# Attention by two key tiles: scores in runs of three, two and three, and a third place for the probabilities

## The chip, the cores and the metric

The kernel runs on one core of one Trainium2 chip. The metric is the device time of one execution in microseconds, the median of several; lower is better. A separately profiled execution gives the trace that the rows below are read from.

## The reference, cut to what matters

One transformer layer on x of 2 x 1024 x 256, float32: half a feed-forward block (with a product-key expert part), then attention with 16 heads of width 16, then half a feed-forward block again. The change is in the attention:

```python
q, k, v = (_split(lora_linear(layernorm(x), W, b, Bm, Am)) for each of q, k, v)   # 2 x 16 x 1024 x 16
scores = jnp.einsum('bhqd,bhkd->bhqk', q, k) * 16 ** -0.5
attn = jax.nn.softmax(scores, axis=-1)
out = jnp.einsum('bhqk,bhkd->bhqd', attn, v)
x = x + lora_linear(out, Wo, bo, Bo, Ao)
```

## The kernel before

The heads are taken two at a time: 16 groups (g) of two heads (j = 0, 1), eight groups for each of the two batches. A group has 1024 queries and 8 key tiles (kt) of 128 keys.

**Stacks.** For every head, q and k are split into a high and a low float32r part and stacked into 48 rows, so that one matmul over 48 rows gives an exact enough score. Head 0's rows stand in partitions 0 to 48, head 1's in partitions 64 to 112, so that matmuls of the two heads use different halves of TensorE's rows. Row 49 of each (index 48) is one row more: minus the maximum of the query on q's side, ones on k's side. So the maximum of each query must be known before the scores proper of its group can be computed.

**Max pairs.** The maxima of group g + 1 are prepared during group g. `max_scores(g, m)` computes one of 16 pairs: two matmuls (`max_pair`, L1595), head 1 and then head 0, each 128 queries by 512 keys, into two banks of `max_ps`. VectorE then takes the maximum over both banks in one instruction (`take_maxima`, L1865). `max_ps` holds two pairs, so pair m may start when the reduce of pair m - 2 has ended (the wait on `pair_max`, L1602). `ahead(g, step)` issues pair step + EARLY of the coming group; EARLY is 6.

**Scores.** `score(g, i)` (L1635) is one of 32 matmuls of a group: 128 keys by 512 queries, i // 4 the key tile, i % 2 the head. It writes one of three banks, the ring (`score_ps`, RING = 3): element n waits for ScalarE to have emptied element n - 3 (`ring_slot`). ScalarE's `exponential` (L1785) turns a bank into probabilities in `probs`, which has two places, one for each key tile.

**Value products.** `mix(g, kt, part)` (L1654) multiplies values and probabilities of a key tile for half of the queries. It is four float32 matmuls with 32 columns of weights and 256 moving columns each, which take one quarter of TensorE's columns each; the trace shows eight, since each float32 matmul is issued as two. `mixed_ps` sums them over the eight key tiles. After the last key tile ScalarE copies it out (`copy_mixed`, L1790), and the first value product of the next group waits for that copy.

**The order on TensorE** is written out by hand. A key tile kt of group g is

```python
score(g, 4 * kt)
ahead(g, 2 * kt)
score(g, 4 * kt + 1)
mix(*divmod(g * KEY_TILES + kt - 1, KEY_TILES), 0)
score(g, 4 * kt + 2)
ahead(g, 2 * kt + 1)
score(g, 4 * kt + 3)
mix(*divmod(g * KEY_TILES + kt - 1, KEY_TILES), 1)
```

so half a key tile is a run of four wide matmuls (score of head 0, max pair head 1, max pair head 0, score of head 1) and then four value products. In front of some key tiles stand other ring elements: the transposes of the group before (`turn_out`, L1623, at kt 2), the turn of the maxima (`turn_group_max`, L1616, at kt 6), and from group 9 on the output projection of the first batch (`attention_rows` at kt 3, `output_product`, L356, at kt 5). In the last group the turns and routing rows of the second feed-forward stand there too. The other engines follow the same order, the ring's by `PLACE`, a table made from `ring_order`.

**Weights.** The weights of the second feed-forward are fetched again during the attention into `weights_again` (L208, on the SP queue) and split by GpSimd (L233, L235); that tensor has two places of 1024 columns.

Of the kernel before, what the change touches and what calls it, by code (L numbers as in the profile page):

```python
# [152 lines left out]
class FfnWeights:  # L153
# [61 lines left out]
    def raw_again(self, i, places):  # L215
        place = places[:, i % 2, :]
        if self.AGAIN[i].startswith("late"):
            return place[:, 0:CHUNK]
        return place.rearrange("p (k f) -> p k f", k=KT)
# [194 lines left out]

class LastMix:
# [13 lines left out]
    def copy_on_scalar(self, act, bank):  # L429
        act.wait_ge(self.turned, 1)  # L430
        act.wait_ge(self.group_out, 2 * (GROUPS - 2))
        act.activation(self.rows.rearrange("p t a b -> p (t a b)"), bank, ACT.Copy).then_inc(self.copied, 1)
# [906 lines left out]
def attention_block(nc, block, sem, dram, keep, attn, proj, norm, halves, weights, project, later, later_space):  # L1339
# [4 lines left out]

    KEY_TILES = SEQ // P
    STRIP = 32
    PAIRS = 2 * KEY_TILES
    SCORES = KEY_TILES * 2 * 2
    EARLY, EARLY_IN_FRONT = 6, 4
    RING, PROBS = 3, 2  # L1350
    OUT_TURN_AT, MAX_TURN_AT = 2, 6
    COPY_AFTER = 3
    UPDATE_AT, TURN_ROWS_AT, PRODUCT_AT = 5, 3, 5
    FIRST_PAIR_AT = 9
    NORM_PAIRS = JT // 2
    LATER_TURNS, LATER_ROWS = (1, 2, 3, 4), (3, 4, 5, 6)

    def ring_order():
# [3 lines left out]
        for g in range(GROUPS):  # L1362
            for kt in range(KEY_TILES):
                if kt == OUT_TURN_AT and g:
                    yield "out", g - 1
                if kt == MAX_TURN_AT and g < GROUPS - 1:
                    yield "max", g + 1
                if (g, kt) == (FIRST_PAIR_AT - 1, UPDATE_AT):
                    yield "update", 0
                if kt == TURN_ROWS_AT and 0 <= g - FIRST_PAIR_AT < NORM_PAIRS:  # L1370
                    yield "rows", g - FIRST_PAIR_AT
                if kt == PRODUCT_AT and 0 <= g - FIRST_PAIR_AT < NORM_PAIRS:
                    yield "product", g - FIRST_PAIR_AT
                for i in range(4 * kt, 4 * kt + 4):
# [18 lines left out]
    with ExitStack() as scope:  # L1393
# [13 lines left out]
        again = sb("weights_again", [P, 2, KT * HALF_INTER], F32)  # L1407
# [6 lines left out]
        turned = sb("turned", [P, 2, KEY_TILES // 2, 4, STRIP], F32)  # L1414
# [173 lines left out]
        def _(pe):  # L1588
# [97 lines left out]
            def ahead(g, step):  # L1686

                later, m = divmod(step + EARLY, PAIRS)
                if g + 1 + later < GROUPS:
                    max_scores(g + 1 + later, m)  # L1690
# [16 lines left out]
            def first_key_tile():  # L1707
                for half in range(2):
                    score(0, 2 * half)
                    max_scores(1, EARLY_IN_FRONT + 2 * half)  # L1710
                    score(0, 2 * half + 1)
                    value_rows(TILES - 2 + half)
                    max_scores(1, EARLY_IN_FRONT + 2 * half + 1)
# [18 lines left out]
            for m in range(EARLY_IN_FRONT):  # L1732
# [3 lines left out]
                value_rows(10 + m)  # L1736
            for g in range(GROUPS):
                for kt in range(KEY_TILES):
                    if kt == OUT_TURN_AT and g:
                        turn_out(g - 1)  # L1740
                    if kt == MAX_TURN_AT and g < GROUPS - 1:
                        turn_group_max(g + 1)
                    if (g, kt) == (FIRST_PAIR_AT - 1, UPDATE_AT):
                        out = ring_slot(PLACE["update", 0])
                        pe.wait_ge(project.raw_in, 48)
                        project.update_on_tensor(pe, out).then_inc(ring_in, 1)
                    if kt == TURN_ROWS_AT and 0 <= g - FIRST_PAIR_AT < NORM_PAIRS:
                        attention_rows(g - FIRST_PAIR_AT)
# [253 lines left out]
```

## Time and profile before

| | |
|---|---|
| Median of 3 runs | 835.8 us (833.98 to 836.37) |
| Profiled execution, its own time | 834.09 us |
| Its span in the trace | 832.3 us |
| TensorE matmul busy | 807.2 us, 97% of the span |
| VectorE busy | 684.2 us, 82% |
| ScalarE busy | 472.6 us, 57% |
| Reduces of max pairs (L1865) | 256, 311.1 us busy, 29.7 us idle before them |
| Exponentials (L1785) | 512, 277.2 us busy, 39.3 us idle before them |

Busy time is a sum over the span. The first feed-forward and the projections fill about the first 270 us, the attention the next 355, the second feed-forward the rest. A matmul's bar in the trace has a modelled end, so what counts on TensorE are the distances from start to start.

### The profile page before, as it was taken

The page shows a single profiled execution, that of the slowest core. Times are in us where ns is not written, and L with a number is a line of the kernel's source. Part 1 is how long each engine was busy: PE and PEld are TensorE (multiplying, and loading weights), DVE is VectorE, ACT ScalarE, POOL GpSimd, SP SyncE. Part 2 cuts the span into 40 slices and gives each one's busy share as a digit, 9 for nine tenths or more (in the row PEclk, how much of TensorE's full clock was granted, in tenths as well). Part 3 has the DMA queues.
Part 4 walks back from the last instruction along what each step waited for, and adds up shares of the span by engine and source line. Part 5 has one row for each costly group of instructions (what it writes and reads, how often), then busy time and mean ns, then how long its engine had stood idle before and what let it go on. Part 6 is the DMA issues. An engine that isn't in the chain of part 4 may idle for free.

```text
span 832.3 us, 14311 instructions
## 1 busy us (share of the span) xinstructions
PE 807.2 (97%) x5424; PEld 516.6 (62%) x5424; DVE 684.2 (82%) x1130; ACT 472.6 (57%) x897; POOL 189.5 (23%) x203
## 2 busy tenths in 40 slices
PE   5989999999999999999999999999999999999997
PEld 4868788887876433333333444443358888888886
DVE  5998798787699999999999988889846977876865
ACT  4444333342442788888888888888863333333322
POOL 2450212021011033333332421143430201120100
PEclk9999999999999999999999999999999999999999
DMA  8110000000050242223333222210000000000000
GB/s 288 41 27 1 0 1 1 1 2 0 1 90 1 40 78 54 40 39 65 65 65 64 41 39 40 57 35 26 15 14 1 1 2 26 0 26 1 1 25 26
DMA packets 19333, 27.87 MB, mean 33 GB/s; under 512 B 4608, under 2 KB 13632, under 8 KB 19264
## 3 DMA queue, kind: packets, MB, share of 16 engines
q1 hardware_dynamic: 18784, 26.40, 14.4%
q8 instruction: 43, 0.70, 0.4%
q10 hardware_dynamic: 480, 0.56, 0.3%
q14 instruction: 26, 0.21, 0.1%
HBM read 12.09 MB, written 2.10 MB: 17 GB/s over the span
## 4 chain that ended last, share of the span: by engine, by line
PE 85%; DVE 8%; ACT 4%; issue 2%; DMA 1%; DVEq 0%; ACTq 0%; POOL 0%
PE front_ps L1654 16%; PE front_ps L1635 13%; PE max_ps L1595 6%; PE ffn_gate_ps L48 5%; PE ffn_gate_ps L50 5%; PE ffn_gate_ps L49 5%; PE ffn_out_ps L741 5%; PE ffn_out_ps L742 5%; PE ffn_out_ps L745 5%; PE ffn_up_ps L48 3%; PE ffn_up_ps L49 3%; PE ffn_up_ps L50 3%; ACT probs L1785 2%; PE ffn_mix_ps L720 2%; DVE ffn_hidden_lo L1103 1%
## 5 line engine op out<-in xcount | busy, mean ns | idle before, releaser
L1865 DVE TENSOR_REDUCE maxima<-max_ps 128x2 f32<-128x1024 f32 x256 | 311.1, 1223 | 29.7 <-PE max_ps L1595 26.9
L1785 ACT ACTIVATE probs<-front_ps 128x512 f32<-128x512 f32 x512 | 277.2, 597 | 39.3 <-PE front_ps L1635 29.5
L873 ACT ACTIVATE ffn_tanh<-ffn_gate_ps 128x512 f32<-128x512 f32 x96 | 57.4, 598 | 227.5 <-PE ffn_gate_ps L50 227.5
L1654 PE MATMUL front_ps<-probs,values 128*32 128x256 f32 x2048 | 163.4, 391 | 4.5 <-ACT mixed_t L1790 4.0
L1112 DVE SCALAR_TENSOR_TENSOR ffn_gated<-ffn_tanh,ffn_gate_ps 128x512 f32<-128x512 f32 x96 | 65.7, 685 | 61.6 <-ACT ffn_tanh L873 61.2
L1654 PEld LDWEIGHTS front_ps<-probs,values 128*32 128x32 f32 x2048 | 40.8, 107 | 95.3 <-issue 55.7
L1635 PE MATMUL front_ps<-q_stack,k_stack 49*128 49x512 f32 x256 | 94.7, 446 | 0.0
L1595 PE MATMUL max_ps<-ffn_xlo,ffn_xhi 48*128 48x512 f32 x256 | 93.8, 447 | 0.0
L1635 PE MATMUL front_ps<-ffn_xhi,ffn_xlo 49*128 49x512 f32 x256 | 91.6, 456 | 0.0
L1535 POOL TENSOR_TENSOR inverse_sum<-turned,minus_one 128x16 f32<-128x16 f32 x15 | 43.7, 2912 | 207.6 <-ACT turned L1797 207.6
L1595 PE MATMUL max_ps<-k_stack,q_stack 48*128 48x512 f32 x256 | 88.2, 455 | 0.6 <-DVE maxima L1865 0.4
L48 PE MATMUL ffn_gate_ps<-ffn_xhi,block 128*128 128x512 f32 x192 | 78.1, 407 | 1.4 <-DVE ffn_xlo L1014 1.4
L741 PE MATMUL ffn_out_ps<-ffn_hidden_hi,block 128*128 128x512 f32 x192 | 78.9, 411 | 0.0
L50 PE MATMUL ffn_gate_ps<-ffn_xlo,block 128*128 128x512 f32 x192 | 76.0, 396 | 0.0
L49 PE MATMUL ffn_gate_ps<-ffn_xhi,block 128*128 128x512 f32 x192 | 75.7, 394 | 0.0
L742 PE MATMUL ffn_out_ps<-ffn_hidden_hi,block 128*128 128x512 f32 x192 | 75.1, 391 | 0.0
L1103 DVE TENSOR_TENSOR ffn_hidden_lo<-ffn_hidden,ffn_hidden_hi 128x512 fp32r<-128x512 f32 x96 | 72.6, 757 | 0.2
L1635 PEld LDWEIGHTS front_ps<-q_stack,k_stack 49*128 49x128 f32 x256 | 39.0, 185 | 47.3 <-ACT probs L1785 43.9
L1635 PEld LDWEIGHTS front_ps<-ffn_xhi,ffn_xlo 49*128 49x128 f32 x256 | 38.1, 184 | 47.1 <-ACT probs L1785 39.0
L956 POOL TENSOR_TENSOR ffn_mix<-ffn_row_exp,ffn_expo 128x512 f32<-128x512 f32 x32 | 34.5, 1099 | 139.7 <-DVE ffn_row_exp L1080 139.7
L879 ACT ACTIVATE ffn_hidden_hi<-ffn_hidden 128x512 fp32r<-128x512 f32 x96 | 59.8, 623 | 3.4 <-DVE ffn_hidden L1124 1.9
L745 PE MATMUL ffn_out_ps<-ffn_hidden_lo,block 128*128 128x512 f32 x192 | 59.6, 391 | 1.4 <-DVE ffn_hidden_lo L1103 1.4
(205 smaller groups left out, 1287.0 us busy)
## 6 DMA issues: line engine op xcount, KB each, us to landing
q_stack<-block SPq DMA_DIRECT2D x48, 64.0 KB, 2.3
ffn_xhi<-block SPq DMA_DIRECT2D x48, 64.0 KB, 2.3
ffn_xlo<-block SPq DMA_DIRECT2D x48, 64.0 KB, 2.3
k_stack<-block SPq DMA_DIRECT2D x42, 64.0 KB, 2.3
x_sb<-in_x SPq DMA_DIRECT2D x3, 512.0 KB, 9.0
out<-x_sb SPq DMA_DIRECT2D x3, 512.0 KB, 2.9
ffn_out_rows<-in_down SPq DMA_DIRECT2D x4, 256.0 KB, 6.2
weights_again<-in_gate SPq DMA_DIRECT2D x2, 512.0 KB, 3.6
```

Of the source, the lines that this page charges most:

```text
L48: pe.matmul(out, w_hi, x_hi, start=(k == 0), stop=False)
L49: pe.matmul(out, w_lo, x_hi, start=False, stop=False)
L50: done = pe.matmul(out, w_hi, x_lo, start=False, stop=(k == last))
L741: pe.matmul(out_ps[:, k, :], weights.late_hi(piece)[:, at], x_hi, start=(m == 0), stop=False)
L742: pe.matmul(out_ps[:, k, :], weights.late_lo(piece)[:, at], x_hi, start=False, stop=False)
L745: out = pe.matmul(out_ps[:, k, :], weights.late_hi(piece)[:, at], x_lo, start=False, stop=(m == UNITS - 1))
L1103: v.tensor_tensor(hidden_lo[:, u % SPLIT_RING, :], hidden[:, u % HIDDEN_RING, :], hidden_hi[:, u % SPLIT_RING, :].bitcast(F32), ALU.subtra ...
L1595: return pe.matmul(max_ps[:, m % 2, j, :], q_stack[s][rows, qt * P:(qt + 1) * P], k_stack[s][rows, half * HALF:(half + 1) * HALF], start=T ...
L1635: pe.matmul(out, k_stack[s][rows, kt * P:(kt + 1) * P], q_stack[s][rows, half * HALF:(half + 1) * HALF], start=True, stop=True).then_inc(r ...
L1654: mm = pe.matmul(mixed_ps[strip:strip + STRIP, at:at + HALF // 2], values[g % SLOTS][:, kt, j, :], probs[:, (g * KEY_TILES + kt) % PROBS, ...
L1785: act.activation(probs[:, tile % PROBS, j, half * HALF:(half + 1) * HALF], score_ps[:, n % RING, :], ACT.Exp, scale=SCORE_SCALE).then_inc( ...
L1865: v.reduce_max(maxima[:, g % 2, m // 2, m % 2, :], max_ps[:, m % 2, :, :], axis=AXIS_X).then_inc(pair_max, 1)
```

## The change

The attention is now issued by two key tiles at a time (`two`, four of them in a group). The eight scores of two key tiles stand in runs of three, two and three. One max pair is split at each of the two inner borders: its head 1 matmul ends a run and its head 0 matmul begins the next, so that the runs have six, four and six wide matmuls. A value product of four stands behind the first and the second run, and two of them (of the first of the two key tiles) behind the third. `probs` has three places. The other ring elements stand in front of the run of two. EARLY is 8 instead of 6. To make room, `turned` is stored with 17 columns of each strip of 32 (ScalarE's copies read only those), and `weights_again` has one place for the four wide pieces and two for the narrow ones, so a wide piece is fetched when the one before it is split.

```diff
@@ load_again, sp
-        if i >= 2:
-            sp.wait_ge(self.again_lo, i - 1)
+        if i:
+            sp.wait_ge(self.again_lo, i if i <= 4 else max(i - 1, 4))
@@ used_columns (new), and its use
+def used_columns(bank):
+    return bank.rearrange("p (s x) -> p s x", x=STRIP)[:, :, 0:HD + 1]
...
-                act.activation(turned[:, g % 2, :, :, :].rearrange("p t a b -> p (t a b)"), score_ps[:, n % RING, :],
-                               ACT.Copy).then_inc(ring_out, 1)
+                act.activation(turned[:, g % 2, :, :, :].rearrange("p t a b -> p (t a) b"),
+                               used_columns(score_ps[:, n % RING, :]), ACT.Copy).then_inc(ring_out, 1)
@@ constants and storage
-    EARLY, EARLY_IN_FRONT = 6, 4
-    RING, PROBS = 3, 2
-    OUT_TURN_AT, MAX_TURN_AT = 2, 6
-    COPY_AFTER = 3
-    UPDATE_AT, TURN_ROWS_AT, PRODUCT_AT = 5, 3, 5
+    EARLY, EARLY_IN_FRONT = 8, 5
+    RING, PROBS = 3, 3
+    TWOS = KEY_TILES // 2
+    TURN_ROWS_AT, OUT_TURN_AT, MAX_TURN_AT, PRODUCT_AT = range(TWOS)
+    UPDATE_AT = PRODUCT_AT
...
-    LATER_TURNS, LATER_ROWS = (1, 2, 3, 4), (3, 4, 5, 6)
+    LATER_TURNS, LATER_ROWS = (2, 4, 6, 8), (5, 7, 9, 10)
...
-        again = sb("weights_again", [P, 2, KT * HALF_INTER], F32)
+        again = sb("weights_again", [P, KT, HALF_INTER], F32)
...
-        turned = sb("turned", [P, 2, KEY_TILES // 2, 4, STRIP], F32)
+        turned = sb("turned", [P, 2, KEY_TILES // 2, 4, HD + 1], F32)
@@ the order of the ring
+            for two in range(TWOS):
+                for i in range(8 * two, 8 * two + 3):
+                    yield "score", (g, i)
...
-                for i in range(4 * kt, 4 * kt + 4):
+                for i in range(8 * two + 3, 8 * two + 8):
                     yield "score", (g, i)
@@ TensorE
-            def max_scores(g, m):
-                if m == 0:
+            def max_scores(g, m, heads=(1, 0)):
+                if g >= GROUPS:
+                    return
+                if m == 0 and 1 in heads:
                     pe.wait_ge(stacks_in[g % SLOTS], (g // SLOTS + 1) * STACK_DMAS * 16)
-                if g * PAIRS + m >= 2:
+                if g * PAIRS + m >= 2 and 1 in heads:
                     pe.wait_ge(pair_max, g * PAIRS + m - 1)
-                max_pair(g, m, 1)
-                max_pair(g, m, 0).then_inc(pair_scored, 1)
+                for j in heads:
+                    scored = max_pair(g, m, j)
+                    if j == 0:
+                        scored.then_inc(pair_scored, 1)
...
+            def two_key_tiles(g, two):
+                i, step, last_group = 8 * two, 4 * two, g == GROUPS - 1
+                tile = g * KEY_TILES + 2 * two
+                score(g, i)
+                ahead(g, step)
+                score(g, i + 1)
+                score(g, i + 2)
+                ahead(g, step + 1, (1,))
+                if last_group:
+                    run_later(3 * two)
+                mix(*divmod(tile - 1, KEY_TILES), 0)
+                between(g, two)
+                ahead(g, step + 1, (0,))
+                score(g, i + 3)
+                score(g, i + 4)
+                ahead(g, step + 2, (1,))
+                if last_group:
+                    run_later(3 * two + 1)
+                mix(*divmod(tile - 1, KEY_TILES), 1)
+                ahead(g, step + 2, (0,))
+                score(g, i + 5)
+                score(g, i + 6)
+                ahead(g, step + 3)
+                score(g, i + 7)
+                if last_group:
+                    run_later(3 * two + 2)
+                mix(g, 2 * two, 0)
+                mix(g, 2 * two, 1)
```

`between` holds the calls of `turn_out`, `turn_group_max`, `attention_rows` and `output_product` that stood in the loop, each now with its own `two`: the rows of the output projection at 0, the turn of the group before at 1, the turn of the maxima at 2, the product and the update of its weights at 3. `run_later` holds those of the second feed-forward. The first two key tiles of group 0 are written out in a new function `first_two`, which mixes their eight scores with seven max pairs and the last two value-row products; five max pairs of group 1 now stand in front of it where four stood before. ScalarE takes its work in the new ring order, with `copy_mixed` behind the exponential of score 4 of a group.

## Rows read from the trace of the kernel before

**Rows 1.** Busy time in one group; columns: window, its length, busy us (instructions) by engine

```profile
338.85:359.86 21.01, 20.73 (x199) 8.11 (x197) 19.59 (x18) 18.44 (x35) 6.73 (x5) 1.00 0.24 40
```

**Rows 2.** Chain that ended last, 317 to 341 us; start, length, what

```profile
317.88 1.09 ACT probs L1785 x2
...
338.85 1.08 ACT probs L1785 x2
```

**Rows 3.** Timeline of TensorE's matmuls, 355.55 to 358.10 us; start, length, what

```profile
355.61 0.50 PE L1635 MATMUL front_ps<-ffn_xhi,ffn_xlo 49*128 49x512 f32 x1
355.61 0.73 PE L1595 MATMUL max_ps<-k_stack,q_stack 48*128 48x512 f32 x2
355.95 0.40 PE L1635 MATMUL front_ps<-ffn_xhi,ffn_xlo 49*128 49x512 f32 x1
356.28 0.64 PE L1654 MATMUL front_ps<-probs,values 128*32 128x256 f32 x8
356.85 0.50 PE L1635 MATMUL front_ps<-ffn_xhi,ffn_xlo 49*128 49x512 f32 x1
```

**Rows 4.** Timeline of TensorE's weight loads, the same stretch

```profile
355.72 0.19 PEld L1635 LDWEIGHTS front_ps<-ffn_xhi,ffn_xlo 49*128 49x128 f32 x1
```

**Rows 5.** Groups of instructions by shape, 300 to 440 us; busy, mean ns, idle before

```profile
L1865 DVE TENSOR_REDUCE maxima<-max_ps 128x2 f32<-128x1024 f32 x107 | 130.1, 1223 | 8.7 <-PE max_ps L1595 7.6
L1785 ACT ACTIVATE probs<-front_ps 128x512 f32<-128x512 f32 x214 | 116.1, 596 | 14.9 <-PE front_ps L1635 10.5
```

**Rows 6.** Timeline of TensorE's matmuls, 274.6 to 275.6 us, group 0's first key tile

```profile
274.97 0.62 PE L1635 MATMUL front_ps<-q_stack,k_stack 49*128 49x512 f32 x2
...
275.52 0.39 PE L1302 MATMUL front_ps<-wv_hi,ffn_xhi 128*128 128x256 f32 x1
```

**Rows 7.** Timeline of TensorE's matmuls, 623.9 to 625.7 us, end of the attention

```profile
624.24 1.07 PE L1654 MATMUL front_ps<-probs,values 128*32 128x256 f32 x16 [0.42 <-ACT probs L1785]
625.24 0.50 PE L48 MATMUL ffn_gate_ps<-ffn_xhi,block 128*128 128x512 f32 x1
```

**Rows 8.** Timeline of VectorE in two windows, around 277 us and 288 us

```profile
276.31 1.22 DVE L1865 TENSOR_REDUCE maxima<-max_ps 128x2 f32<-128x1024 f32 x1
...
288.38 2.35 DVE L1865 TENSOR_REDUCE maxima<-max_ps 128x2 f32<-128x1024 f32 x2
```

**Rows 9.** Timeline of TensorE (272.5 us on) and of VectorE (270.4 us on)

```profile
272.54 0.73 PE L1595 MATMUL max_ps<-k_stack,q_stack 48*128 48x512 f32 x2
...
273.31 1.22 DVE L1865 TENSOR_REDUCE maxima<-max_ps 128x2 f32<-128x1024 f32 x1 [0.33 <-PE max_ps L1595]
```

**Rows 10.** Timeline of TensorE's weight loads, 276.2 to 278.3 us

```profile
276.44 0.19 PEld L1595 LDWEIGHTS max_ps<-k_stack,q_stack 48*128 48x128 f32 x2 [0.15 <-DVE maxima L1865]
...
277.58 0.18 PEld L1595 LDWEIGHTS max_ps<-k_stack,q_stack 48*128 48x128 f32 x2 [0.83 <-DVE maxima L1865]
```

**Rows 11.** Timeline of weight loads and of matmuls, 588.3 to 589.8 us

```profile
588.70 0.18 PEld L1635 LDWEIGHTS front_ps<-ffn_xhi,ffn_xlo 49*128 49x128 f32 x1
...
589.12 0.64 PE L1654 MATMUL front_ps<-probs,values 128*32 128x256 f32 x8
```

**Rows 12.** Timeline of TensorE's matmuls at the border of two groups, 339.8 us on

```profile
339.90 0.40 PE L1635 MATMUL front_ps<-ffn_xhi,ffn_xlo 49*128 49x512 f32 x1
340.57 0.64 PE L1654 MATMUL front_ps<-probs,values 128*32 128x256 f32 x8 [0.28 <-ACT mixed_t L1790]
```

**Rows 13.** Timeline of TensorE's matmuls, 592.1 us on, key tile 5 of group 14

```profile
592.17 0.50 PE L1635 MATMUL front_ps<-ffn_xhi,ffn_xlo 49*128 49x512 f32 x2
...
594.41 0.28 PE L1616 MATMUL front_ps<-ident,maximum 128*16 128x128 f32 x1
```

**Rows 14.** Instructions on `weights_again`; duration ns min/median/max, first and last start

```profile
L235 POOL TENSOR_TENSOR block<-weights_again,block x12: 1278/1282/2378, 391.2 to 611.9; 128x512 fp32r<-128x512 f32 x8, 128x1024 fp32r<-128x1024 f32 x4
L208 SPq DMA_DIRECT2D weights_again<-in_gate x2: 437/437/437, 375.9 to 396.9; - x2
```

More of the change, by code:

```diff
@@ L215, in raw_again @@
     def raw_again(self, i, places):
[L216 to L219, printed above, removed]
+        return places[:, i % 2, :] if self.AGAIN[i].startswith("late") else places[:, :, :]
     def wait_again(self, pe, piece):
@@ L431, in copy_on_scalar @@
         act.wait_ge(self.group_out, 2 * (GROUPS - 2))
-        act.activation(self.rows.rearrange("p t a b -> p (t a b)"), bank, ACT.Copy).then_inc(self.copied, 1)
+        act.activation(self.rows.rearrange("p t a b -> p (t a) b"), used_columns(bank), ACT.Copy
+                       ).then_inc(self.copied, 1)
     def write_on_vector(self, v):
@@ L1684, in rows_later, with ahead @@
                              .rearrange("p h k -> p (h k)"))
-            def ahead(g, step):
+            def ahead(g, step, heads=(1, 0)):
                 later, m = divmod(step + EARLY, PAIRS)
-                if g + 1 + later < GROUPS:
-                    max_scores(g + 1 + later, m)
+                max_scores(g + 1 + later, m, heads)
             def product(m):
@@ L1705, in value_rows, with first_two @@
                 proj.value_rows_on_tensor(pe, t, front_bank("rows", t // 2))
[L1707 to L1713, printed above, removed]
+            def first_two():
+                early = iter(range(EARLY_IN_FRONT, EARLY + 4))
+                score(0, 0)
+                max_scores(1, next(early))
+                score(0, 1)
+                score(0, 2)
+                max_scores(1, next(early))
+                value_rows(TILES - 2)
+                max_scores(1, next(early))
+                score(0, 3)
+                score(0, 4)
+                max_scores(1, next(early))
+                value_rows(TILES - 1)
+                max_scores(1, next(early))
+                score(0, 5)
+                max_scores(1, next(early))
+                score(0, 6)
+                max_scores(1, next(early))
+                score(0, 7)
+                mix(0, 0, 0)
+                mix(0, 0, 1)
@@ new lines, in run_later, with between @@
+            def run_later(run):
+                if run in LATER_TURNS:
+                    turn_later(LATER_TURNS.index(run))
+                if run in LATER_ROWS:
+                    rows_later(LATER_ROWS.index(run))
+            def between(g, two):
+                if two == OUT_TURN_AT and g:
+                    turn_out(g - 1)
+                if two == MAX_TURN_AT and g < GROUPS - 1:
+                    turn_group_max(g + 1)
+                if (g, two) == (FIRST_PAIR_AT - 1, UPDATE_AT):
+                    out = ring_slot(PLACE["update", 0])
+                    pe.wait_ge(project.raw_in, 48)
+                    project.update_on_tensor(pe, out).then_inc(ring_in, 1)
+                if two == TURN_ROWS_AT and 0 <= g - FIRST_PAIR_AT < NORM_PAIRS:
+                    attention_rows(g - FIRST_PAIR_AT)
+                if two == PRODUCT_AT and 0 <= g - FIRST_PAIR_AT < NORM_PAIRS:
+                    output_product(g - FIRST_PAIR_AT)
@@ L1850, in _ @@
                         ring_copy(("product", r), project.rows[:, (r + 1) % 2, :])
-                    for i in range(4 * kt, 4 * kt + 4):
+                    exponential(g, 8 * two + 3)
+                    exponential(g, 8 * two + 4)
+                    if two == 0 and g:
+                        copy_mixed(g - 1)
+                    elif two == 0:
+                        value_rows(7)
+                    for i in range(8 * two + 5, 8 * two + 8):
                         exponential(g, i)
-                        if i == COPY_AFTER and g:
-                            copy_mixed(g - 1)
-                        elif i == COPY_AFTER:
-                            value_rows(7)
             copy_mixed(GROUPS - 1)
```

61 lines of the change are left out of this document (19 added, 42 removed).

## The prediction

> **What bounds the kernel now.** I read the busy time by stage first, then the chain that ended last, then the timeline of one steady stretch. Within a group of the attention TensorE is busy 20.73 of 21.01 us, VectorE 19.59, ScalarE 18.44 [rows 1]: three engines near full, so a gain on one is small unless the others follow. The chain runs from group to group in 20.97 us (317.88 to 338.85) [rows 2] and passes through TensorE, save once a group through two exponentials and the copy. VectorE waits for TensorE 7.6 us in 140 [rows 5]. So TensorE sets the pace.
>
> Half a key tile takes 1.24 us, 355.61 to 356.85 [rows 3]. The matmuls of the two heads stream together; I call two such a slot. The first slot starts at 355.61, the second 0.34 later at 355.95, because its weights are only loaded from 355.72 on [rows 4]; the value products start 0.33 after that and the next run 0.57 after them. Two key tiles are four such halves, 4.96 us; 16 halves are 19.84 of the group's 20.97. The rest, 1.13, is the wait of the first value product for `copy_mixed`, which starts 0.67 after the slot in front of it instead of 0.33 [rows 12], so 0.34, and 0.79 for the turns.
>
> **TensorE's side of the change.** A third slot in a run starts 0.23 after the second (the second of two scores starts at 0.62 - 0.39), while another shape starts 0.32 after the last slot [rows 6]. A run of six is thus 0.34 + 0.23 + 0.33 = 0.90, the run of four 0.67. One value product stays 0.57; two in a row are 1.00 (624.24 to 625.24) instead of 1.14 [rows 7]. Two key tiles: 0.90 + 0.57 + 0.67 + 0.57 + 0.90 + 1.00 = 4.61 us, 0.35 less than 4.96.
>
> A rule that agrees: by the Trainium skill, TensorEngine Tiling (Array Packing), Key Properties, going from one tiling mode to another drains the engine, and the change has three such exchanges where there were four. By that rule alone the change is worth what TensorE saves.
>
> **VectorE's side.** The reduces need 1.13 us from start to start when nothing is late (2.35 - 1.22) [rows 8], 4.52 for the four of two key tiles. That is under 4.61, but with 2% to spare and only two places, and now the pairs no longer come evenly. Let c be the start of the third run. It begins with head 0 of the third pair, the fourth pair stands at its end, so both are scored within 0.5 us; then comes none until the next run's second slot. The second pair is opened at the end of the first run and closed only behind the value products, and holds a place for that time.
>
> The hand-overs: a reduce starts 0.04 after the matmul's bar ends (272.54 + 0.73 = 273.27, reduce at 273.31) [rows 9], so 0.54 after the start of a first slot (bar 0.50). A freed place is used 0.05 after the reduce's end (276.31 + 1.22 = 277.53, load at 277.58) [rows 8, 10]. A matmul whose weight load comes late, in the middle of a run, holds the next shape back until 0.42 after that load (588.70 to 589.12) [rows 11].
>
> The chain of waits then closes on itself. From c: 0.54 to the third pair's reduce, 1.13 to the fourth's, 1.22 to its end, 0.05 to the load of head 1 of the next second pair (which needs the fourth's place), 0.42 to the value products, 0.57 to the run of two, and 0.67 + 0.57 = 1.24 to the next c. The sum is 5.17 us, against 4.61 without it. TensorE would want that load 2.36 after c (0.34 + 0.23 + 0.33 + 1.00 for the third run and its products, 0.46 into the next) and gets it at 2.94.
>
> A second loop goes through the other waits. From the run of two, b: 0.54 + 1.22 + 0.05 until head 1 of the fourth pair may load, 0.11 for that load (355.61 to 355.72) [rows 3, 4], 0.23 + 0.33 + 1.00 to the next period, 0.34 + 0.43 to its first pair's reduce, 1.22 + 0.05 until the next third pair may load, 0.42 + 0.57 to c: 6.51. With c to b by the first loop (3.93) that is 10.44 for two periods, 5.22. I take T = 5.20 for two key tiles; the bounds are 5.12 (the hand-overs at their shortest) and 5.30.
>
> A rule that bears on it: by the Trainium skill, TensorEngine Tiling (Array Packing), PSUM Bottleneck, packing speeds up TensorE and not the emptying of PSUM, which can become the bottleneck. It speaks against the change in the same sense as the loops.
>
> **The other edits.** `copy_mixed` now has the third run to hide behind: its copy (0.60, like an exponential [rows 5]) ends before the two value products at c + 0.90, so the 0.34 goes; uncovered it costs 0.34 again. The turns and the output projection keep their matmuls and still follow a value product: 0.79 a group and unchanged elsewhere. The third place of `probs` takes a wait from ScalarE, which is not late: 8 exponentials at 0.49 (1.09 - 0.60) [rows 2, 5] are 3.92 of 5.2. The narrower copy of the turns shortens work off the path; nothing to 0.2 us a group, taken as nothing. The single wide place of `weights_again`: a split that starts at 391.2 ends at 393.6, and the next load is issued at 396.9 [rows 14], so SP waits for nothing; if it did, the stacks of a group three ahead stand behind it. Front: seven pairs in `first_two` at 1.13 are 7.9 us for VectorE, but VectorE is idle before them now (0.33 and more [rows 9]) and a pair is moved ahead; between -0.6 and +2.3 (two pairs more), taken as 0.
>
> **Sum.** A new group is 4 x 5.20 + 0.79 = 21.59 against 20.97: +0.62, times 13 groups, +8.1. Group 0 has three such periods instead of six key tiles at 2.48: +0.7. At the end, pairs are needed until key tile 4 of group 14 now and until 3 with EARLY 8; after that a key tile without pairs takes 2.24 (592.17 to 594.41) [rows 13]. New, a period without pairs is bound by the ring: from c, 0.54 + 2 x 0.49 + 0.60 + 0.05 until score 2 of the next may load, 0.42 + 0.57 + 0.42 + 0.57, is 4.15, and about 0.2 for score 4, which waits for the exponential of score 1: 4.35. Now: 5 x 2.48 + 11 x 2.24 + 2 x 0.34 = 37.7; new: 2 x 5.20 + 6 x 4.35 = 36.5; -1.2. In all +7.6, or 57 T - 288.8 in general. The profiled execution took 834.1, so 842; it is 1.7 below the median 835.8, which goes to 843.5. I forecast 844.
>
> **Rivals.**
> Faster: TensorE's saving arrives, because VectorE's waits overlap and only its sum counts. T = 4.61, 57 T - 288.8 = -26, 810 us. For it: 4.52 is under 4.61, and TensorE is the bound. Against it: program order. It decides if the first loop is under 5.02; it is 5.17 by eight rows, and no single one is off by 0.15 likely. 15%. The rule on the drain is on this side.
> No change: the late load costs only its lateness, since the slot's weights would be exposed in part anyway; 0.33 instead of 0.42 in each loop gives about 5.08, +0.8, 837 us. 11%.
> Slower still: the ring's waits add to those of the pairs, as in the stretch without pairs (0.2 a period): T = 5.40, +19, 855 us. For it: three scores in a row want all three banks. Against it: ScalarE has 1.3 us to spare in each period. 12%.
> The forecast itself: 62%, its own range 840 to 849.
>
> **Numbers.** A measurement here tells about 0.3%, 2.5 us, from no change. Faster 15%, same 11%, slower 62 + 12 = 74%. The range goes from 831 (some way into the first two rivals) to 853.
>
> **What the profile would show.** Between groups 21.6 us on the chain instead of 20.97, with VectorE's reduces on it, which are not on it now. TensorE idle, or its weight loads waiting for the reduces, at two places of a period: in front of the value products of the first run and in the third run, about 0.5 us and 0.3 us. A third slot 0.23 behind the second. No wait for `copy_mixed`. The reduces in twos: third and fourth back to back at 1.13, the second alone. Periods of 4.6 us would prove me wrong; so would a weight load of a pair that starts before the reduce that frees its place, or a stretch without pairs that is not faster.

## The result and the profile after

The changed kernel takes 845.8 us (median of 4, 843.84 to 847.09), the kernel before, on the same chip, 834.9: a ratio of 1.0132, with a 95% interval of 1.0115 to 1.0150, so 11 us slower. Its profiled execution took 846.68 us, its span is 844.9.

The page of the changed kernel first: the span, the busy time by engine, the chain by engine, and the groups of the reduces and of the exponentials.

```profile
span 844.9 us, 14310 instructions
PE 822.4 (97%) x5424; PEld 546.9 (65%) x5424; DVE 678.6 (80%) x1130; ACT 463.7 (55%) x897; POOL 189.7 (22%) x203
...
PE 87%; DVE 8%; issue 2%; ACT 1%; DMA 1%; DVEq 0%; ACTq 0%; POOL 0%
...
L1923 DVE TENSOR_REDUCE maxima<-max_ps 128x2 f32<-128x1024 f32 x256 | 306.6, 1221 | 43.7 <-PE max_ps L1604 37.5
L1839 ACT ACTIVATE probs<-front_ps 128x512 f32<-128x512 f32 x512 | 271.8, 601 | 59.3 <-PE front_ps L1648 56.0
```

The work is the same (256 reduces of 1.22 us), but VectorE now sits idle 37.5 us for the max matmuls, where it was 26.9 us in the kernel before:

```profile
L1865 DVE TENSOR_REDUCE maxima<-max_ps 128x2 f32<-128x1024 f32 x256 | 311.1, 1223 | 29.7 <-PE max_ps L1595 26.9
```

Where TensorE's time went shows in the chain of the stretch of 315 to 345 us. Its columns are start, length and what; shown are the pair of value products that ends a period of two key tiles, and, one group on, every piece of the period up to the next such pair.

```profile
320.12 1.00 PE front_ps L1667 x16
...
336.57 1.00 PE front_ps L1667 x16
337.57 0.43 PE front_ps L1648
338.00 0.24 PE max_ps L1604 x2
338.24 0.24 PE front_ps L1648 x2
338.48 0.29 PE max_ps L1604
338.77 0.57 PE front_ps L1667 x8
339.34 0.43 PE max_ps L1604
339.76 0.23 PE front_ps L1648 x2
339.99 0.05 PE max_ps L1604
340.04 0.57 PE front_ps L1667 x8
340.61 0.42 PE max_ps L1604
341.04 0.24 PE front_ps L1648 x2
341.27 0.31 PE max_ps L1604 x2
341.58 0.23 PE front_ps L1648
341.81 1.00 PE front_ps L1667 x16
```

A group is 341.81 - 320.12 = 21.69 us, against 20.97 [rows 2]; a period without turns is 341.81 - 336.57 = 5.24. No reduce stands on this chain: it puts the lost time down to `max_ps` on TensorE. The busy time of one group, in the window view, hides it too:

```profile
318.10:339.80 21.70, 21.70 (x199) 10.09 (x197) 19.35 (x17) 17.85 (x35) 6.73 (x5) 1.00 0.22 38
```

TensorE is busy 21.70 of 21.70, where it was 20.73 of 21.01 [rows 1]: the modelled bars of its matmuls cover the gaps. The gaps show in the distances from start to start, and their cause in the weight loads and in VectorE's lane. This is the timeline of the next period, TensorE's matmuls, then its loads, then VectorE:

```profile
342.74 0.50 PE L1648 MATMUL front_ps<-ffn_xhi,ffn_xlo 49*128 49x512 f32 x1
343.09 0.61 PE L1648 MATMUL front_ps<-ffn_xhi,ffn_xlo 49*128 49x512 f32 x2
343.91 0.64 PE L1667 MATMUL front_ps<-probs,values 128*32 128x256 f32 x8
344.48 0.50 PE L1604 MATMUL max_ps<-k_stack,q_stack 48*128 48x512 f32 x1
345.22 0.64 PE L1667 MATMUL front_ps<-probs,values 128*32 128x256 f32 x8
345.79 0.50 PE L1604 MATMUL max_ps<-k_stack,q_stack 48*128 48x512 f32 x1
346.96 0.64 PE L1667 MATMUL front_ps<-probs,values 128*32 128x256 f32 x8
...
343.48 0.18 PEld L1604 LDWEIGHTS max_ps<-k_stack,q_stack 48*128 48x128 f32 x1 [0.21 <-DVE maxima L1923]
344.79 0.18 PEld L1604 LDWEIGHTS max_ps<-k_stack,q_stack 48*128 48x128 f32 x1
346.29 0.19 PEld L1604 LDWEIGHTS max_ps<-k_stack,q_stack 48*128 48x128 f32 x2 [0.21 <-DVE maxima L1923]
...
341.07 3.66 DVE L1923 TENSOR_REDUCE maxima<-max_ps 128x2 f32<-128x1024 f32 x3
345.01 2.54 DVE L1923 TENSOR_REDUCE maxima<-max_ps 128x2 f32<-128x1024 f32 x2 [0.28 <-PE max_ps L1604]
```

The run of three and a head, 342.74 to its value products at 343.91, takes 1.17 us instead of the 0.90 of the sum; the run of two, 344.48 to 345.22, 0.74 instead of 0.67; the third run, 345.79 to 346.96, 1.17 instead of 0.90. These 0.61 us are the difference between the 4.61 of TensorE alone and the 5.22 that a period takes. Each of the three late loads begins 0.05 to 0.06 behind the end of a reduce: 341.07 + 1.14 + 1.22 = 343.43 and 343.48 (the second of three in a row, which started 1.14 behind the first), 341.07 + 3.66 = 344.73 and 344.79, 345.01 + 1.22 = 346.23 and 346.29. The value products stand 0.43 behind two of these loads (343.48 to 343.91, 344.79 to 345.22), and 0.67 behind the one that has a slot of scores behind it (346.29). The waits of 290 to 620 us, with columns of total, times and longest, say the same in two directions, and none is for `mixed_t`:

```profile
DVE maxima L1923 <- PE max_ps L1604: 37.0, 56, 2.2
...
PEld max_ps L1604 <- DVE maxima L1923: 25.4, 111, 0.3
```

**Where the 12.6 us lie** (spans 844.9 and 832.3; by the starts of the first score of each group in the two traces). 1.85 lie ahead of the first max pair, in instructions that both kernels share; that point falls between 240.1 and 243.5 us over the kernels below, so it is scatter of one execution. From the first pair of group 1, which is scored in front of group 0, to the second period of group 0 (the front): +1.6, 14.48 for 12.86. Rest of group 0: +0.8. Groups 1 to 13: +8.9, 0.685 each. Group 14 +0.3, group 15 -0.6, after the attention -0.2.

### The profile page after: what moved, and what is told of

It reads as the page before. It is cut to its first block, busy times and chain, and to the rows that moved or that the text cites. A ratio compares the mean times of both kernels' runs of the same rounds, so it can differ in the third digit from the quotient of the medians.

```text
span 844.9 us, 14310 instructions
## 1 busy us (share of the span) xinstructions
PE 822.4 (97%) x5424; PEld 546.9 (65%) x5424; DVE 678.6 (80%) x1130; ACT 463.7 (55%) x897; POOL 189.7 (22%) x203
## 4 chain that ended last, share of the span: by engine, by line
PE 87%; DVE 8%; issue 2%; ACT 1%; DMA 1%; DVEq 0%; ACTq 0%; POOL 0%
PE front_ps L1667 16%; PE max_ps L1604 12%; PE front_ps L1648 11%; PE ffn_gate_ps L48 5%; PE ffn_gate_ps L50 5%; PE ffn_gate_ps L49 5%; PE ffn_out_ps L747 5%; PE ffn_out_ps L748 4%; PE ffn_out_ps L751 4%; PE ffn_up_ps L50 3%; PE ffn_up_ps L48 3%; PE ffn_up_ps L49 3%; PE ffn_mix_ps L726 2%; DVE ffn_hidden_lo L1109 1%; DVE maxima L1923 1%
## 5 line engine op out<-in xcount | busy, mean ns | idle before, releaser
L1923 DVE TENSOR_REDUCE maxima<-max_ps 128x2 f32<-128x1024 f32 x256 | 306.6, 1221 | 43.7 <-PE max_ps L1604 37.5
L1839 ACT ACTIVATE probs<-front_ps 128x512 f32<-128x512 f32 x512 | 271.8, 601 | 59.3 <-PE front_ps L1648 56.0
L1667 PE MATMUL front_ps<-probs,values 128*32 128x256 f32 x2048 | 150.1, 388 | 0.4 <-ACT probs L1839 0.4
L1667 PEld LDWEIGHTS front_ps<-probs,values 128*32 128x32 f32 x2048 | 47.0, 108 | 67.9 <-issue 33.9
L1648 PE MATMUL front_ps<-q_stack,k_stack 49*128 49x512 f32 x256 | 90.2, 434 | 0.0
L1648 PE MATMUL front_ps<-ffn_xhi,ffn_xlo 49*128 49x512 f32 x256 | 87.9, 443 | 0.2 <-ACT probs L1839 0.2
L1604 PEld LDWEIGHTS max_ps<-ffn_xlo,ffn_xhi 48*128 48x128 f32 x256 | 37.7, 184 | 36.5 <-issue 20.4
L1604 PEld LDWEIGHTS max_ps<-k_stack,q_stack 48*128 48x128 f32 x256 | 34.8, 183 | 36.0 <-issue 18.3
```

The costliest lines, as they stand in the source:

```text
L1604: return pe.matmul(max_ps[:, m % 2, j, :], q_stack[s][rows, qt * P:(qt + 1) * P], k_stack[s][rows, half * HALF:(half + 1) * HALF], start=T ...
L1648: pe.matmul(out, k_stack[s][rows, kt * P:(kt + 1) * P], q_stack[s][rows, half * HALF:(half + 1) * HALF], start=True, stop=True).then_inc(r ...
L1667: mm = pe.matmul(mixed_ps[strip:strip + STRIP, at:at + HALF // 2], values[g % SLOTS][:, kt, j, :], probs[:, (g * KEY_TILES + kt) % PROBS, ...
L1839: act.activation(probs[:, tile % PROBS, j, half * HALF:(half + 1) * HALF], score_ps[:, n % RING, :], ACT.Exp, scale=SCORE_SCALE).then_inc( ...
L1923: v.reduce_max(maxima[:, g % 2, m // 2, m % 2, :], max_ps[:, m % 2, :, :], axis=AXIS_X).then_inc(pair_max, 1)
```

## The experiments

Ratios are to the kernel before, timed on the same chip in turn. Group times are from the first score of a group to that of the next, groups 1 to 7.

### 1. Half of each reduce, with the new order and with the old

The maxima are taken over half of the columns, so the output is not the reference's; everything else is issued as it was. One edit, made in the changed kernel (`after_half_reduce`) and in the kernel before (`before_half_reduce`):

```diff
-                v.reduce_max(maxima[...], max_ps[:, m % 2, :, :], axis=AXIS_X
+                v.reduce_max(maxima[...], max_ps[:, m % 2, :, 0:HALF // 2], axis=AXIS_X
```

> The changed kernel with each reduce of a max pair over half of the columns (256 of 512 in each bank); the maxima leave out half of the keys. A reduce then takes about 0.69 us instead of 1.22. If the reduces' two loops set the period of two key tiles (5.2 us), both fall below TensorE's own sum and the period becomes 4.61: 26 us under the kernel before by the formula of the prediction, about 809 us, a group near 19.2 us, and no weight load of a max pair waits for VectorE. If the ring of three score banks or TensorE's own split runs set it, the period stays above 5 us and the time above 832 us.

> The kernel before with the same halved reduces (the maxima leave out half of the keys), as a control. VectorE does not set its period, so the reduces' theory says no change: 835 us within 2 us, half a key tile at 1.24 us as before. If the reduces cost time there too, it falls by several us.

Measured: changed kernel 822.7 us, ratio 0.9859 (0.9846 to 0.9873); kernel before 833.3, ratio 0.9993 (0.9979 to 1.0006). A group of the changed kernel fell from 21.69 to 19.75, the group of the kernel before did not move (20.97 and 20.96). No weight load of a pair waits for VectorE any more in the changed kernel between 300 and 440 us, as expected. The chain of the changed kernel with short reduces, 290 to 400 us:

```profile
314.87 1.00 PE front_ps L1667 x16
319.51 1.00 PE front_ps L1667 x16
...
329.50 1.00 PE front_ps L1667 x16
334.62 1.00 PE front_ps L1667 x16
```

A period without turns is 319.51 - 314.87 = 4.64, close to the 4.61 summed for TensorE; 329.50 to 334.62, with 0.21 of a turn in it, is 4.91 without that turn, and the one at the group's border 4.76. Those two wait for the ring (for the turn of the maxima, and for ScalarE, which copies `mixed`); that in the changed kernel the waits for the reduces cover this is an inference, and experiment 6 fits it. So the reduces carry the loss within the groups: the old order does not wait for them there, the new one does. In front of them both orders wait: with short reduces the front of the kernel before falls from 12.86 to 11.91 us, about the 1 us by which its total fell, and that of the changed kernel from 14.48 to 12.66. The total missed the expected 809 by 14 us, for the ring, and for one more thing, told under what was unexpected.

### 2. Whole pairs, and one whole pair

`whole_pairs` keeps the new runs but scores both heads of every pair together, behind the value product; `second_pair_whole` does that for the second pair of a period alone (the first two lines of the edit).

```diff
-                ahead(g, step + 1, (1,))
...
-                ahead(g, step + 1, (0,))
+                ahead(g, step + 1)
...
-                ahead(g, step + 2, (1,))
...
-                ahead(g, step + 2, (0,))
+                ahead(g, step + 2)
```

> The changed kernel with both split pairs whole at the start of the next run: runs of five, four and seven wide matmuls. The second pair no longer asks for its place before the fourth's reduce has ended, the third none before the first's. TensorE needs nine slots instead of eight, 4.61 + 0.23 = 4.84 us; the head 1 matmul of the fourth pair may still come 0.1 late. Reduce theory: period 4.84 to 4.95, a group about 20.4 us, 826 to 831 us, faster than both kernels. If split pairs do not matter and the extra slot only adds, the period is 5.2 + 0.23 and the time about 858 us. If the ring sets the period, no change from 846 us.

> The changed kernel with only one of its two split pairs whole again: both matmuls of the second pair of maxima of a period stand behind the first run's value products, those of the third pair stay on either side of the second run's. My theory, two loops of waits of about equal length (5.17 and 5.22 us a period), of which this edit opens the one that runs through the second pair and loosens the other: a period of about 5.1, a group of 21.2, and 838 to 840 us in all. Rival A (only the second loop, through the third pair, binds): groups stay at 21.6 and the time at 845. Rival B (only the first binds): groups as with both whole, 20.8, and 835 us.

Measured: `whole_pairs` 834.5 us, ratio 0.9999 (0.9989 to 1.0009), a group of 20.77; `second_pair_whole` 841.0 us, 1.0075 (1.0061 to 1.0088), a group of 21.36. Whole pairs take the loss away, but the 826 to 831 us and the gain over the kernel before that were expected did not come: the group is 0.4 above the expected 20.4, and the front stays as long as in the changed kernel (14.45). With whole pairs the loads' waits for the reduces fall to 5.6 us in the stretch of 300 to 440 us, from 12.0. Undoing both splits gives 0.92 a group back, undoing one 0.33: neither rival with one loop alone holds (21.6 or 20.8), and the total of the second is 1 us above the range that was given.

### 3. Whole pairs with half of each reduce

The edits of 1 and 2 together. The first set:

> whole_pairs with each reduce over half of the columns (the maxima leave out half of the keys). Theory: in whole_pairs nine slots of TensorE (4.84 us) set the period, with about 0.1 of lateness of the fourth pair. So the group falls from 20.77 only to about 20.4 us and the time by some 3 to 5 us to 830, where the same halving took 23 us off the changed kernel. If the reduces still set the period of whole_pairs, it falls by 10 us or more.

It gave 839.5 to 859.9 us and once 2597. The second set, of the same kernel:

> The changed kernel with whole pairs and with half of each reduce left out (the maxima are taken over half of the keys' scores), once more, unchanged: its first set lay between 839 and 2597 us and gives no verdict. With the reduces out of the way only TensorE's own order and the ring's waits are left. My theory: 4.62 + 0.11 for the slot more, and the same ring waits as in after_half_reduce, a group of about 20.1 and 829 us. Rival (whole pairs cost more than a slot by themselves): over 833. Rival (order does not matter without reduces): 823.

Measured: 858.6 us, ratio 1.0292. The total was missed by 30 us, 28 of them in groups 0 to 2 (93.6 us in place of some 65.7), at a lower clock (below). From group 3 on the group is 20.60, against the 20.1 expected, which had put the slot more at 0.11 a period; it takes 0.21 (a period without turns and without the group's border is 4.85, 422.80 to 427.65 on its chain, against 4.64). That completes a table of group times:

| us a group | pairs split | pairs whole |
|---|---|---|
| reduces of 1.22 us | 21.69 | 20.77 |
| reduces of 0.69 us | 19.75 | 20.60 |

The split is worth 0.85 a group to TensorE (0.21 a period: whole pairs make runs with an odd number of wide matmuls, and the one left over takes a slot of its own) and costs 0.92 where a pair is opened in one run and closed in the next while VectorE needs 1.22 us for each. The same edit is a gain or a loss by the length of the reduce.

### 4. The storage alone

The kernel before with three places of `probs`, the narrow `turned` and the single wide place of `weights_again`.

```diff
-    RING, PROBS = 3, 2
+    RING, PROBS = 3, 3
...
-        again = sb("weights_again", [P, 2, KT * HALF_INTER], F32)
+        again = sb("weights_again", [P, KT, HALF_INTER], F32)
...
-        turned = sb("turned", [P, 2, KEY_TILES // 2, 4, STRIP], F32)
+        turned = sb("turned", [P, 2, KEY_TILES // 2, 4, HD + 1], F32)
```

> The kernel before with the storage edits alone: three places of probabilities, the turned rows at 17 columns a strip, one wide place for the weights fetched again; the order is that of before. Theory: none of them is on the path, 835 us within 2 us. Rival: the narrower copies of the turns or the third place are worth something by themselves (up to 0.2 us a group, 3 us in all), or the single place makes SP late and costs time.

Measured: 834.5 us, ratio 1.0001 (0.9990 to 1.0012), a group of 20.96. Nothing, as forecast.

### 5. The old order, with one new period a group

The storage of experiment 4, the front and EARLY of the kernel before, and only the first two key tiles of a group in runs of three, two and three; `copy_mixed` one score later. In `hybrid_whole` the pairs there are whole, in `hybrid_split` split.

```diff
+            def first_key_tiles(g):
+                score(g, 0)
+                ahead(g, 0)
+                score(g, 1)
+                score(g, 2)
+                mix(g - 1, KEY_TILES - 1, 0)
...
+                ahead(g, 1)
+                score(g, 3)
+                score(g, 4)
+                mix(g - 1, KEY_TILES - 1, 1)
+                ahead(g, 2)
+                score(g, 5)
+                score(g, 6)
+                ahead(g, 3)
+                score(g, 7)
+                mix(g, 0, 0)
+                mix(g, 0, 1)
...
-                        if i == COPY_AFTER and g:
+                        if i == COPY_AFTER + 1 and g:
```

> The order of the kernel before with its storage edits (three places of probabilities), except that the first two key tiles of groups 1 to 15 are issued in the layout of whole_pairs (runs of five, four and seven wide matmuls, value products behind the first two and two behind the third, copy_mixed behind the exponential of score 4). Theory: the only lasting gain in the change is that copy_mixed has a run to hide behind. There the two key tiles take 4.95 us as measured in whole_pairs instead of 4.96 + 0.34, so a group 20.6 us instead of 20.97, 15 times 0.35 is 5 us: 829 to 830 us where before takes 834.5. Rival: the change of layout within a group costs the reduces as much at the border, and nothing changes (834 us).

> As hybrid_whole, but with the two pairs split at the inner borders as in the change (runs of six, four and six). Reduce theory: head 1 of the second pair comes 0.35 us late and head 1 of the fourth 0.34 (each counted from the reduce that frees its place, as in the prediction), so these two key tiles take about 5.27 us, hardly less than the 5.30 of before: 833 to 835 us, and 4 to 5 us more than hybrid_whole in spite of a slot less. If splitting is harmless and only TensorE's slots count, it is the faster of the two by 15 times 0.23, 3.5 us.

> The kernel hybrid_whole once more, unchanged, for a profile of it and a second set of times (its first set gave 829.1 to 832.0 us, with a first execution of 4212 us in which every matmul took some 1.75 us where it takes 0.4 elsewhere). My theory: the groups from 1 on run as in whole_pairs, 20.77 us (no wait of TensorE for the copy of mixed, a wait of some 0.2 a period for the reduces), and the front runs as in before, so the time is 830 to 832 us, 0.4 to 0.6% under before. Rival (the first set was chance): 834 to 835.

Measured: `hybrid_whole` 830.9 us over five executions (a sixth took 4212 us), ratio 0.9950 (0.9936 to 0.9964), and in the second set 830.0, ratio 0.9944 (0.9929 to 0.9958); `hybrid_split` 833.7, ratio 1.0000 (0.9988 to 1.0012). `hybrid_whole` is the only version here that computes what the reference does and beats both kernels. The second set's chain of `hybrid_whole`, 290 to 400 us, at the borders of groups:

```profile
297.87 1.01 PE front_ps L1659 x16
...
318.49 1.01 PE front_ps L1659 x16
```

A group is 20.62 (20.63 by most of the first scores), 0.34 less than 20.97: just the wait for `mixed_t` [rows 12], which the new runs hide. The new period itself takes 4.96 without the turn in it, what two old key tiles take. With the pairs split the group is 20.95: the loads' waits for the reduces, 2.8 us in the stretch of 300 to 440 us against 1.3 with whole pairs and none in the kernel before, take the same 0.3 back, in one period of four.

### 6. More work for ScalarE

The changed kernel with a copy of 128x48 behind every second exponential, to find out whether the ring's waits bound it.

```diff
+                if i % 2:
+                    if g or i > 1:
+                        act.wait_ge(scratch_set, g * SCORES // 2 + i // 2)
+                    act.activation(scratch[:, :], attn["ident"][:, 0:48], ACT.Copy).then_inc(scratch_set, 1)
```

> The changed kernel with a small copy of 48 columns more on ScalarE behind every second exponential (four in two key tiles, some 0.2 us each), which nothing reads. Reduce theory: ScalarE has 1.3 us to spare in a period of 5.2, so 846 us within 2 us. Ring theory (the waits for ScalarE's banks add to those for the reduces): each of them comes straight behind an exponential and holds the next back, 0.2 us a period or more, 11 us: 857 us.

Measured: 847.4 us, ratio 1.0152 (1.0139 to 1.0165), a group of 21.81: 0.12 more than the changed kernel, for 16 copies a group of some 0.24 us each. ScalarE has room, and the rival in which the ring adds to the pairs' waits falls.

### 7. Two pairs less ahead

EARLY is 6 again, and the turn of the maxima and the output product change places.

```diff
-    EARLY, EARLY_IN_FRONT = 8, 5
+    EARLY, EARLY_IN_FRONT = 6, 3
...
-    TURN_ROWS_AT, OUT_TURN_AT, MAX_TURN_AT, PRODUCT_AT = range(TWOS)
+    TURN_ROWS_AT, OUT_TURN_AT, PRODUCT_AT, MAX_TURN_AT = range(TWOS)
...
                if m < 4:
                    value_rows(10 + m)
+            value_rows(13)
```

> The changed kernel with the maxima two pairs less ahead: EARLY 6 instead of 8, three pairs of group 1 in front of the first scores instead of five, and the turn of the maxima moved to the last two key tiles of a group (the product of the output projection takes its place in the third). My theory: of the 12.5 us by which the changed kernel's span is longer, some 2.4 lie between the first pair of group 1 and the end of group 0, because VectorE's reduces are back to back there; two pairs less in front take 2 x 1.13 = 2.3 off, one half period at the end goes back to the pace with pairs (+0.4): 844 us, between 843 and 845, the groups at 21.7 as in the changed kernel. Rival A (the front is bound by TensorE's order in the first two key tiles, not by the reduces): 846 to 847. Rival B (the place of the turn of the maxima matters for the pace, since the two ring elements now stand otherwise): groups off 21.7 by more than 0.2 and a total off by 3 us or more.

Measured: 853.9 us, ratio 1.0214 (1.0194 to 1.0233). The expectation failed: 8 us more than the changed kernel, not less. The groups 1 to 4 are 22.0, groups 5 to 7 are 23.3 to 25.6, and group 13 is 24.7 (21.67 in the changed kernel). By these numbers rival B is nearest, but what the traces show is another cause than the place of the turn. The stretch ahead of group 1 did what was expected of it by half: from the first pair of group 1 to the start of group 1 it takes 29.19 us, the changed kernel 30.36 and the kernel before 27.94, so two pairs give back 1.2 of the 2.4. The chain of this kernel, 310 to 345 us:

```profile
330.21 1.24 DVE maxima L1924
...
331.47 0.03 DVE maximum L1931
...
331.85 2.35 DVE maxima L1924 x2
...
334.25 0.49 PE max_ps L1604
```

After the 16 reduces of a group VectorE takes the larger of each two maxima in one small instruction (`maximum`, L1931 here). With the pairs two less ahead it stands between the second and the third pair of a period. The reduce behind it starts 0.38 later (331.47 to 331.85), another follows without a gap, and the load of the next second pair, at 334.25, stands 0.05 behind their end (331.85 + 2.35 = 334.20). The turn comes 1 us behind that late load. The last period of a group takes 0.3 more than in the changed kernel, where the same instruction costs 0.14 (332.80 to 332.94) behind the fourth pair. And the instruction is not always short. In group 5, on VectorE and then on GpSimd, which splits weights of the second feed-forward:

```profile
397.49 1.56 DVE L1931 TENSOR_TENSOR maximum<-maxima 128x16 f32<-128x16 f32 x1
...
396.62 2.38 POOL L232 TENSOR_TENSOR block<-weights_again,block 128x1024 fp32r<-128x1024 f32 x1
```

It takes 0.19 us with nothing on GpSimd beside it, 0.45 to 0.47 beside another instruction of GpSimd in groups 1 to 4, and 1.56 to 1.58 in groups 5 to 7 and 1.27 in group 13, each time begun inside a split of weights. These are the four stretched groups. In group 5 the granted clock is 1.00 up to 400 us, and 0.80 and then 0.73 only behind it, from 400 to 407 us, so the lower clock follows this wait and does not lead to it. That GpSimd's work makes the instruction long is read from the overlap alone; no run took it away. The place of the turn and the lead of the pairs were moved together, so this run does not price either alone, and nothing in it shows a cost of the turn's place.

## Why the prediction came out right

Forecast 844 us, 840 to 849 by its own range; measured 845.8. The change itself was forecast at 8.2 us (844 less 835.8) and measured at 10.9 (845.8 less 834.9); that the totals lie only 1.8 apart is in part luck, since the kernel before came out 0.9 lower in this comparison.

**TensorE's side** holds. The third slot stands 0.23 behind the second (of the two scores at 343.09 the second starts 0.61 less one bar of 0.39 later, 0.22), two value products take 1.00 (336.57 to 337.57), and with the reduces shortened a period comes to 4.64 against 4.61. The trace agrees with the rule on the drain in the Trainium skill, TensorEngine Tiling (Array Packing), Key Properties, but the exchange is small here: 0.33 from a slot to another shape against 0.23 within a run. Of the 0.35 of TensorE's side, the exchange into the value products is 0.10. The rest also comes from one run less: a first slot at 0.34 became one at 0.23 (0.11), and of two value products in a row the first takes 0.43 (1.00 less 0.57) instead of 0.57 (0.14).

**The first loop** holds link by link. c, the start of the third run, is 340.55 in this trace; the load of head 1 of the second pair is at 343.48, 2.93 later (forecast 2.94), the value products 0.43 behind it (0.42), the run of two after 0.57, and the next c at 345.79, 1.31 later (1.24). The sum is 5.24 against 5.17, and the missing 0.07 is the run of two, 0.74 instead of 0.67: the second loop reaches into it, since head 1 of the third pair waits for the first pair's reduce (344.73, load 344.79). **The second loop** holds too: from b, the start of the run of two, at 344.48 the load came at 346.29, 1.81 later (0.54 + 1.22 + 0.05), and the products 0.67 behind it (0.11 + 0.23 + 0.33). The mean period is 5.22, forecast 5.20; four of them and 0.80 for the turns are 21.69, forecast 21.59, and 13 groups cost 8.9 instead of 8.1. Experiments 1 and 2 show both sides of it: short reduces take the loss away, and so do whole pairs. That within the groups the reduces bound only the new order agrees with the Trainium skill, TensorEngine Tiling (Array Packing), PSUM Bottleneck.

**Where the waits lie** was told in part. Two places were named, of 0.5 and 0.3 us; there are three, of 0.27, 0.07 and 0.27. A wait in the third run shifts what is behind it and so shortens the wait in the first. That the reduces would stand on the chain was wrong: the chain names `max_ps` on TensorE. No wait for `copy_mixed` is left, and `hybrid_whole` prices it at 0.34 a group, as forecast. Of the named signs of being wrong one came in part: a stretch without pairs is faster than one with them, 4.63 against 5.22 a period, but not faster than in the kernel before, which takes 4.50 there.

**The front** was mis-sized: taken as 0 within -0.6 to +2.3, it cost +1.6. The bound from two pairs more was the better value. The sentence that VectorE "is idle before them now" did not carry: in the front it has no idle time left, and TensorE waits for it. From 276 us on it had next to none in the kernel before either. The window view of the kernel before there, and then of the changed kernel:

```profile
276.00:280.00 4.00, 3.60 (x31) 1.50 (x29) 4.00 (x5) 2.93 (x6) 0.00 (x0) 1.00 0.38 61
280.00:284.00 4.00, 4.00 (x42) 1.59 (x40) 3.97 (x4) 3.48 (x7) 0.00 (x0) 1.00 0.61 105
...
272.00:276.00 4.00, 3.59 (x23) 2.40 (x21) 3.90 (x4) 1.89 (x4) 0.00 (x0) 1.00 0.01 2
276.00:280.00 4.00, 3.64 (x22) 2.46 (x23) 4.00 (x5) 1.96 (x5) 0.00 (x0) 1.00 0.00 0
280.00:284.00 4.00, 3.38 (x29) 1.51 (x28) 4.00 (x4) 2.23 (x4) 0.00 (x0) 1.00 0.49 81
```

In the changed kernel VectorE is busy 3.90, 4.00 and 4.00 of 4.00 us, TensorE 3.59, 3.64 and 3.38. Two pairs less ahead give back 1.2 of the 1.6 (14.48 to 13.25 up to the second period of group 0, ahead of the first place that experiment 7 moved the turn from or to). With short reduces the two fronts are 0.75 apart (12.66 and 11.91), so about half of the 1.6 is waiting for reduces. **Group 0** came as forecast (+0.8 for +0.7). **The end** was mis-sized: -0.4 in groups 14 and 15 instead of -1.2. The last period of group 14 takes 4.63, not 4.35, and why was not tested.

So the sum of 7.6 was 3.1 short of the 10.7 that the profiled executions differ by behind the first max pair: 0.8 in the groups, 1.6 in the front, 0.8 at the end, 0.1 in group 0, less 0.2 after the attention. **The storage edits** cost nothing, as `storage_only` shows. Of the rivals, `faster` fails on its deciding point (a first loop under 5.02; it is 5.24), though 1 shows what it would have been with shorter reduces; `no change` fails because the late load does hold the next shape back by 0.43; `slower still` fails on the period (5.22, not 5.40) and by experiment 6.

## What to carry to other kernels

An order that is best for one engine by its own sum can lose to the hand-overs of another whose own sum also fits: write the chain from a freed buffer place to the load that needs it and back, and see whether it closes in less than the period. Do not split a producer of a two-place buffer across other work while its consumer is nearly full; first shorten the consumer, and the same split pays (the table of experiment 3). And take from a large reordering only the piece that removes a wait you can see: the one period with `copy_mixed` behind it was worth 0.5%, the whole change -1.3%. When a lead is moved, look too at what small instructions move with it, and beside which work of another engine they come to stand (experiment 7).

## What was unexpected

With the reduces short, TensorE reached the pairs of group 2 before their stacks had landed and waited 2.4 us and more for that DMA, where the changed kernel waits 0.3. Then its clock fell. These are windows of the changed kernel with half reduces (the column ahead of the last two is the granted clock):

```profile
284.00:288.00 4.00, 1.92 (x21) 0.77 (x19) 1.47 (x3) 2.17 (x4) 0.00 (x0) 1.00 0.44 76
...
292.00:296.00 4.00, 4.00 (x28) 1.73 (x26) 1.38 (x2) 1.62 (x4) 0.00 (x0) 0.50 0.49 82
296.00:300.00 4.00, 4.00 (x40) 2.01 (x42) 2.06 (x4) 3.26 (x7) 0.00 (x0) 0.93 0.58 97
```

and of the kernel with whole pairs and half reduces, second set:

```profile
284.00:288.00 4.00, 1.63 (x18) 0.60 (x17) 1.02 (x3) 1.94 (x4) 0.00 (x0) 1.00 0.34 60
...
292.00:350.00 58.00, 58.00 (x324) 24.18 (x321) 18.49 (x27) 29.14 (x57) 6.70 (x5) 0.50 0.27 47
```

TensorE was busy 1.92 and 1.63 of 4 us before the clock fell to 0.50, 1.2 GHz. In the first kernel it was back at 2.4 GHz within some 8 us, in the second only after 350 us of the span, some 60 us later, though TensorE's bars had no gap in all that time; in one execution of that kernel's first set (839.5 us) it was back at about 315 us. At the low level group 1 took 35.8 us instead of 20.6. What lets it rise so much later in one run than in another was not found. The three traces with such a wait (2.4, 2.5 and 2.6 us on TensorE) all show the fall, and the changed kernel, which waits 0.3, stays at 1.00 there; that the wait brought it on is read from this order alone. So behind a wait of 2.6 us stood a loss of 28 us: a kernel that is sped up ahead of a DMA can lose more to the clock than to the wait.
